# Two attention stages of a two-layer decoder: transposes issued one batch early, a similarity that ends one batch late, and new issue orders for two streams

## What is computed

```
qkv = (x @ W_qkv).reshape(B, N, 3, H, D)          # H 16 heads of D 16
q, k, v = qkv[:, :, 0], qkv[:, :, 1], qkv[:, :, 2]
q_n  = q[:, REG:] / norm(q[:, REG:])              # REG = 5 register tokens
sim  = (qg_n * q_n).sum(-1).mean(-1)              # likeness to a guide vector
sim  = (sim - sim.min()) / (sim.max() - sim.min())  # over all batches
pos  = sim > 0.9
x_pos = attend(q, k, v, keys = registers and tokens with pos)
x_neg = attend(q, k, v, keys = registers and tokens without pos)
reg_out = (x_pos[:, :REG] + x_neg[:, :REG]) * 0.5
tok_out = where(pos, x_pos, x_neg)[:, REG:]
return concat(reg_out, tok_out) @ W_proj + b_proj
```

## Time and profile before

| what | value |
|---|---|
| median of 3 runs (lowest to highest) | 1870.96 us (1869.15 to 1871.81) |
| profiled execution, its own time | 1873.72 us |
| its span in the trace | 1871.5 us |
| mean granted TensorE clock | 0.929 of 2.4 GHz |
| PE busy | 1573.7 us (84%) |
| DVE busy | 973.5 us (52%) |
| ACT busy | 639.9 us (34%) |
| POOL busy | 433.5 us (23%) |

### The profile page before, as it was taken

The page is one execution under the profiler, slowest core; times in us unless marked ns, Lnnn a source line. Parts: engine busy times, 40 slices in busy tenths (PEclk is TensorE's granted clock), DMA queues, the critical chain, the costliest instruction groups (busy, mean ns, idle before and its releaser), DMA issues.

```text
span 1871.5 us, 29566 instructions
## 1 busy us (share of the span) xinstructions
PE 1573.7 (84%) x12928; PEld 1288.5 (69%) x12928; DVE 973.5 (52%) x1774; ACT 639.9 (34%) x710; POOL 433.5 (23%) x403
## 2 busy tenths in 40 slices
PE   6898999988899999999669968977977982787785
PEld 5787888877688888888647756755864762455453
DVE  4666667665353333333455564565655443565654
ACT  4444534344322332322134424424423420323322
POOL 2220202102233443533302320331250232000000
PEclk9999999999789999999889989989989985879878
DMA  5000000000400010100000000000000001101000
GB/s 210 1 1 1 1 1 1 1 1 15 188 18 18 18 34 18 34 1 1 1 1 1 18 18 1 1 34 1 1 34 1 1 17 68 52 1 52 7 13 12
DMA packets 8625, 42.09 MB, mean 22 GB/s; under 512 B 1073, under 2 KB 3377, under 8 KB 7473
## 3 DMA queue, kind: packets, MB, share of 16 engines
q1 hardware_dynamic: 8496, 40.21, 5.7%
HBM read 31.82 MB, written 8.39 MB: 21 GB/s over the span
## 4 chain that ended last, share of the span: by engine, by line
PE 65%; DVE 21%; ACT 7%; POOL 3%; issue 3%; DMA 1%; SPq 0%; DVEq 0%; POOLq 0%; ACTq 0%
PE ps L111 14%; PE ps L112 13%; PE ps L113 13%; DVE sm L1219 8%; PE ps L519 4%; PE ps L793 4%; DVE m L1208 4%; PE ps L524 3%; PE ps L811 3%; ACT m L1124 3%; PE ps L531 3%; PE ps L651 2%; PE ps L817 2%; ACT m L951 2%; PE ps L635 2%
## 5 line engine op out<-in xcount | busy, mean ns | idle before, releaser
L951 ACT ACTIVATE m<-ps 128x1024 f32<-128x1024 f32 (+5 forms) x232 | 179.9, 800 | 416.2 <-PE ps L113 226.1
L1219 DVE TENSOR_REDUCE sm<-ps 128x8 f32<-128x2048 f32 (+1 forms) x128 | 195.8, 1530 | 87.1 <-PE ps L793 74.2
L1208 DVE TENSOR_TENSOR m<-m,ps 128x1024 f32<-128x1024 f32 (+1 forms) x80 | 91.1, 1139 | 219.3 <-PE ps L113 190.3
L519 PE MATMUL ps<-cst,m 128*77 128x128 f32 (+2 forms) x1008 | 144.7, 289 | 53.5 <-DVE m L1599 24.7
L519 PEld LDWEIGHTS ps<-cst,m 128*77 128x77 f32 (+2 forms) x1008 | 120.0, 152 | 83.2 <-issue 32.4
L1746 POOL TENSOR_TENSOR r<-m,r 128x1024 fp32r<-128x1024 f32 x48 | 115.2, 2401 | 264.4 <-ACT r L951 264.4
L1124 ACT ACTIVATE m<-ps 128x2048 f32<-128x2048 f32 x64 | 119.2, 1876 | 164.0 <-PE ps L811 164.0
L1679 POOL TENSOR_SCALAR sm<-sm 128x2 f32<-128x2 f32 x40 | 8.9, 223 | 646.7 <-DVE sm L1237 646.7
L111 PE MATMUL ps<-xTall,uw 128*128 128x512 f32 x384 | 152.5, 397 | 6.4 <-DVE xres L1208 5.0
L112 PE MATMUL ps<-xTall,uw 128*128 128x512 f32 x384 | 152.0, 396 | 0.0
L113 PE MATMUL ps<-xTall,uw 128*128 128x512 f32 x384 | 151.2, 394 | 0.0
(11 more groups left out here) (179 smaller groups left out, 3749.3 us busy)
## 6 DMA issues: line engine op xcount, KB each, us to landing
raw<-wu_dram SPq DMA_DIRECT2D x12, 768.0 KB, 4.2
keep_dram<-m SPq DMA_DIRECT2D x8, 768.0 KB, 3.3
m<-keep_dram SPq DMA_DIRECT2D x8, 768.0 KB, 4.2
w1raw<-w_dram SPq DMA_DIRECT2D x1, 3840.0 KB, 14.5
w0raw<-w_dram SPq DMA_DIRECT2D x3, 1024.0 KB, 19.4
w1f<-w1f_dram SPq DMA_DIRECT2D x1, 2048.0 KB, 18.9
out_dram<-xres SPq DMA_DIRECT2D x16, 128.0 KB, 1.8
w0f<-w0f_dram SPq DMA_DIRECT2D x1, 1536.0 KB, 14.3
```

What stands on the lines that cost most here:

```text
L519: return pe.transpose(o, i, ident[0:n, 0:n])
L951: return act.activation(o, i, ACT.Copy)
L1208: return dve.tensor_tensor(o, a, b_, op)
L1219: return dve.tensor_reduce(o, i, AX.X, op, **kw)
```

## The change

1. **LAST, early transposes.** A generator `early(st, b)` on PE and ACT issues the first part of batch b+2 within the end of batch b: half of the q heads (`tqa`, into bank 3) behind t3, `tk` behind oT, the other q heads and `xt` behind y. The product y goes to bank 2 in place of bank 1. A batch then begins with `xm`, behind `add` of the stream's batch before.
2. **LAST, registers ahead of scores.** `xo` stands behind t2, ahead of s0, and its copy goes from DVE to ACT. The transpose of it has a signal of its own (`x3`). DVE runs xr, xn, xc ahead of rc and on; xc halves as it copies, and one instruction `ov` adds half of the ordinary rows. `oh` is gone.
3. **SECOND, the similarity ends in the next batch.** `likeness` (sc, sim) of batch b-2 is issued behind the rotary embedding of batch b; the last two batches end it in place. POOL's clearing of the head tiles of b+2 (`blank`) stands in `fq(b)` ahead of bias and pow.
4. **SECOND, split transposes.** The transposes of token half 0 wait for t0 alone, the rest for t1. The first values product `v0` of `xattn` stands between oT and y of `a1`.
5. **Both cross attentions.** DVE runs sums 0, sums 1, shift 2, shift 3 in place of sums 0, shift 2, sums 1, shift 3. `maxima_of` and `attend` have no slot end ahead of their first step.
6. **All order tables are new.** Those of PE in LAST, then `early` on PE, and DVE's `likeness`, its place in `a1`, and the new `ov`:

```
 LAST = {
-    "PE": [12, 12, 12, 13, 13, 15, 15, 15, 16, 16, 18, 19, 20, 21, 22, 22, 23, 23, 24, 24, 25, 26, 30, 31, 36, 38, 39, 40],
+    "PE": [5, 5, 6, 6, 6, 7, 8, 10, 11, 12, 14, 14, 16, 16, 18, 20, 22, 23, 23, 25, 25, 27, 27, 30, 30],
...
+            def early(st, b):
+
+                v, sig, act_, dve_ = f_views(st, b), st.f_pe, st.f_act, st.f_dve
+                pe.wait_ge(*st.f_pool.at("clean"))
+                pe.wait_ge(*dve_.at(b, "f"))
+                turn_heads(bank(st, 3), v, 0, [0, 1], [0, 1]).then_inc(sig.up(b, "tqa"), 1)
+                yield
+                if b >= 2:
+                    pe.wait_ge(*dve_.at(b - 2, "on"))
+                turn_heads(pair(st, 0), v, 16, G4, [0, 1]).then_inc(sig.up(b, "tk"), 1)
+                yield
+                pe.wait_ge(*act_.at(b, "Tk"))
+                turn_heads(bank(st, 1), v, 8, [0, 1], [0, 1]).then_inc(sig.up(b, "tq"), 1)
+                pe.wait_ge(*dve_.at(b, "xq"))
+                for c in range(4):
+                    m = tp(bank(st, 0)[:, 32 * c:32 * c + 8], v.qs[:, 4 * c:4 * c + 4, :].rearrange("p h n -> p (h n)"), 8)
+                m.then_inc(sig.up(b, "xt"), 1)
...
+            def likeness(st, b):
+                sig, qq, dq = st.q_dve, k2(st.sm[:, 32:64]), k2(st.sm[:, 64:96])
+                dve.wait_ge(*st.q_pool.at(b, "pow"))
+                tt(dq, dq, qq, ALU.mult).then_inc(sig.up(b, "sc"), 1)
+                yield
+                dve.wait_ge(*sig.at(b, "sc"))
+                reduce(sim[:, 2 * b:2 * b + 2], dq, ALU.add).then_inc(sig.up(b, "sim"), 1)
...
                     tt(v.QK[:, j, :, 0:16], v.t1[:, j, :, :], v.t2, ALU.add).then_inc(sig.up(b, f"t{j}"), 1)
                 yield
+                yield from likeness(st, b - 2) if b >= 2 else pause(1)
+                yield
                 yield from maxima_of(st, b, v, sig, pe_)
...
-                dve.wait_ge(*sig.at(b, "xc"))
-                tt(ov, ov, v.os[0:REG, :, :], ALU.add).then_inc(sig.up(b, "ov"), 1)
-                dve.wait_ge(*sig.at(b, "ov"))
-                ts(v.o[0:REG, 0, :], v.o[0:REG, 0, :], 0.5, None, ALU.mult).then_inc(sig.up(b, "oh"), 1)
+                dve.wait_ge(*sig.at(b, "on"))
+                stt(ov, ov, 0.5, v.os[0:REG, :, :], ALU.mult, ALU.add).then_inc(sig.up(b, "ov"), 1)
```

More of the change, by code:

```diff
@@ L44 @@
+    "POOL": [4, 4, 4, 4, 10, 10, 12, 13, 13, 13, 13, 13, 15, 16, 17, 17, 17],
 }
 SECOND = {
[L46 to L47 removed]
@@ L55 @@
+    "DVE": [4, 5, 5, 5, 6, 7, 9, 11, 13, 14, 15, 15, 15, 16, 16, 20, 20, 22, 22, 22, 25, 30, 31, 31, 31, 31, 31],
 }
@@ L1181, in fa @@
                 v, sig, pe_, dve_ = f_views(st, b), st.f_act, st.f_pe, st.f_dve
[L1182 to L1187 removed]
+                if b < 2:
+                    for _ in early(st, b):
+                        pass
                 yield
@@ L1191, in fa @@
                 yield
+                act.wait_ge(*pe_.at(b, "xo"))
+                copy(v.ox_[:, :, 0:8], bank(st, 0)[:, 0:32].rearrange("p (c n) -> p c n", c=4)).then_inc(sig.up(b, "xo"), 1)
                 yield
                 yield from attend(st, b, v, sig, pe_)
+                nxt = early(st, b + 2) if b + 2 < B else iter(())
+                yield
+                next(nxt, None)
                 yield
@@ L1333, in xattn @@
                 sums(0)
+                sums(1)
                 shift(2)
-                sums(1)
                 shift(3)
@@ L1535, in fq @@
                 yield
-                dve.wait_ge(*st.q_pool.at(b, "pow"))
-                tt(dq, dq, qq, ALU.mult).then_inc(sig.up(b, "sc"), 1)
-                yield
-                dve.wait_ge(*sig.at(b, "sc"))
-                reduce(sim[:, 2 * b:2 * b + 2], dq, ALU.add).then_inc(sig.up(b, "sim"), 1)
+                if b + 2 >= B:
+                    for _ in likeness(st, b):
+                        pass
                 yield
@@ L1776, in a1, with blank @@
             def a1(st, b):
+                sig = st.a_pool
+                yield from blank(st, b) if b < 2 else pause(1)
+                yield
+                add_bias(st, b, part(w1f, P1F, "bao"), st.a_pe, sig)
+                yield
+                yield from norm_only(st, b + 2) if b + 2 < B else pause(4)
+                yield from layernorm(st, b, st.a_dve, sig)
+                yield
+            def blank(st, b):
                 v, sig = a_views(st), st.a_pool
@@ L1787, in a1 @@
                 z.then_inc(sig.up(b, "z"), 1)
-                yield
-                add_bias(st, b, part(w1f, P1F, "bao"), st.a_pe, sig)
-                yield
-                yield from norm_only(st, b + 2) if b + 2 < B else pause(4)
-                yield from layernorm(st, b, st.a_dve, sig)
-                yield
             def fq(st, b):
@@ L1797, in fq @@
                 qq = k2(st.sm[:, 32:64])
+                yield
+                yield from blank(st, b + 2) if b + 2 < B else pause(1)
                 yield
```

182 lines of the change are left out of this document (106 added, 76 removed).

## The result

The changed kernel takes 1793.58 us (median of 4 runs, 1792.77 to 1799.51) against 1870.06 for the kernel before (4 runs, 1862.82 to 1871.81). The ratio is 0.9605, 95% interval 0.9572 to 0.9638: 4% faster, 76 us by the medians, where 63 were forecast. The predicted 1808 is 14 above the measured time, inside the range and inside the likeliest case's own. All times and ratios here are of fast runs; experiment E6 had two slow ones more (2647.0 and 2926.1 us at a granted clock of 0.55 and 0.81), which are left out.

What follows compares the result with a forecast made beforehand. Chains of waits were taken to bound LAST, and SECOND partly. SECOND -35, LAST -27 and FIRST -1 made -63 on the profiled 1873.7, so 1810.7, or 1808 us by the median; range 1782 to 1848.

Steps and rivals of the forecast that it cites:

- likeliest case: Whole kernel: the gains come as laid out, 1808 us, with a range of its own of 1790 to 1826; chance 0.55.
- SECOND, -35: SECOND: pairs of 145 us instead of 153.3 and the last pair's lag gone (-16); bounds -15 to -54.
- The layout: SECOND's pair from its first x transposes: maxima turned at 41, attention to 60, y at 67, 76.7 of PE work left.
- the 8 us of the order: SECOND: shortening of a pair by the in-step order, 153.3 to 145; waits freed by `likeness` were not added.
- LAST, -27: LAST: pairs of 69, 65 and 65 us from xm to xm, last stretch 71.7; bounds -11 to -42.
- two streams side by side fit into 4.77: Attention steps: both streams' steps come back after 4.77 us like one stream's alone, four steps in 19.1 us.
- the 4 us set aside for the clock: LAST: 4 us added to the 60 to 61 laid out for a pair at the higher clock, giving 65.
- FIRST, -1: FIRST: reordered sums and shifts and a few PE products gain 1 us; bounds -5 and +5.
- Rival B: SECOND: like beside like gives nothing, the period stays 153 and only the end gains (-15): 1828 us; chance 0.17.
- C: SECOND and LAST: short steps with waits run at the lower clock, 28 to 35 us lost: about 1840; chance 0.13.
- E: SECOND and LAST: granted clock falls to 1.2 GHz in nearly all attention steps, kernel slower: 1877 us; chance 0.07.
- D: SECOND: late `pow` holds DVE's maxima some 4 us in each of four pairs: 1823 us; chance 0.05.

Runs made afterwards that it cites:

- E6: Kernel before, with the new LAST and SECOND's old code run with its streams in step; FIRST as before: 1869.0 us (ratio 1.0016).
- E4: Changed kernel, but every similarity ends in its own batch, order tables kept: 1836.8 us (ratio 0.9827).
- E11: Changed kernel, but POOL's clearing of the head tiles is back at the start of self attention, behind `pow`: 1824.5 us (ratio 0.9760).
- E5: Changed kernel, but SECOND's two streams in the order of the kernel before, stream 1 half a batch behind: 1851.7 us (ratio 0.9930).
- E1: Kernel before with the change in LAST alone (early transposes, registers ahead of scores, new order tables there): 1853.2 us (ratio 0.9930).
- E3: Changed kernel, but FIRST's order tables and the order of sums and shifts in both cross attentions as before: 1803.3 us (ratio 0.9646).

## Why the prediction was right, and where its sum was off

- **What bounds it**: right. Chains of waits bounded LAST and in part SECOND, and three quarters or more of the gain are idleness of PE (39.7 of 52.7 us in SECOND, 19.4 of 24.2 in LAST). The rest is shorter busy time, which went with a higher granted clock; the sum counted no gain of that kind.
- **The sum as a whole**: by the spans -79.9 for the forecast -63. SECOND gave 17.7 more than its term, LAST 2.8 less, and the part up to SECOND 2.7 more, which is within the scatter of that place; 0.7 was lost between the stages.
- **SECOND, -35, measured -52.7.** This is the term that was mis-sized. The layout put the end of y at 67; its own parts behind the attention steps add up to 5.9, not 7, so it stood at 66. The attention steps began at 40.9 (laid out: 41) but took 22.0 and not 19.1, and y ended at 69.1. That is 2 us worse than laid out. Against it, PE had by then done 54.9 us of the pair's work, not 50, and the pair's PE time was 124.6, not 126.7, so 69.6 were left and not 76.7: pairs of 140.6 and 139.9, not 145. The first pair gained 2.3 and did not lose 1, and the fourth (160.2 with an end of some 20) gained about 9 and not 4. The end itself was right: 35.7 to 20.
- **`likeness` and `blank`, counted at nothing beside the order**: wrong as a price, right in the sum. The forecast took their waits as part of the 8 us of the order. E4 and E11 show 38 and 28 us in SECOND when one of them is undone, E6 a loss when all are. The layout had them in place, so it came out right; as reasons they stood too low.
- **LAST, -27, measured -24.2.** xm to xm was 68.9, 65.0, 65.6 (laid out: 69, 65, 65) and the last stretch 74.2 and not 71.7. The step "two streams side by side fit into 4.77" failed: 5.39. The pair came out at 65.0 all the same, since the 4 us set aside for the clock happened to cover what went over. Up to the end of the attention steps it took 52.4 for the laid out 48 (30.1 up to s0, at a granted clock of 0.72, and 22.3 behind it, at 1.00); from there to the next xm it took 12.6 for 12 to 13. How much of the 4.4 is the clock is not shown, and the match to the microsecond is partly luck. In the last stretch stream 1's y ended 68.0 behind xm, where the layout has 67, and the residual, norm and store behind it took 6.2, for which the sum left 4.7.
- **FIRST, -1**: no effect that these traces can show.
- **Rival B** (like beside like gives nothing): fell for this code, 140.6 against 153.2 in E5. It holds for the old code in the one order in step that was tried, 160.1 in E6 against 153.3. So the rule of the Trainium skill (Perfetto Trace Analysis, Optimization Strategy), that interleaving regimes of different engines may improve performance, is borne out by the runs only where the chains' gaps stay in the code; with the gaps closed, like beside like is the shorter.
- **C and E** (clock): SECOND was granted 0.95 (before 0.93), LAST 0.84 (before 0.82). No loss in the mean of either stage. **D** (`pow` holds the pair): 14.3 us of waits are left, 11 of them in the last pair, where the similarity is in place.

Not settled: what sets the scatter of LAST's 273.7 to 277.9 us between traces of the same instructions. In E1 and E3, with 277.9 and 276.8, 2.7 and 3.7 of it are in the first pair (71.6 and 72.6 for 68.9), whose first xm took 1.17 us there and 0.73 in the changed kernel, and the granted clock of the stage was 0.82 for 0.84. No run separates cause from effect.

## What to carry to other kernels

Price an order of streams and the code that it runs with together. Here both halves of a change were worth nothing or a loss, in two stages, and the whole was worth 53 and 24 us. The reading that fits the traces: with a lag, one stream's waits are covered by the other's work, and closing them bought nothing (13.9 us fewer waits for `pow` in E5, the same SECOND); in step they are the other stream's waits too. This holds for the orders that were tried; a better one for either half by itself was not looked for. When two streams run in step, look first at every wait that both have at the same place, and at what of the other stream is queued behind it on each engine; an edit there can be worth more than its own length (two waits for `pow`, 11.1 us together, cost 13.5 in E4's second pair; one wait of 5.59 on DVE cost 8 to 10 in E11's).

## What the runs showed that was not expected

- Two streams that alternate the four-step loop in the same banks come back after 5.39 us, where one alone does after 4.77: the engine with two steps in the loop, PE, sets it by its fixed order.
- Where SECOND begins differs by up to 10.1 us (914.5 to 924.6) between executions of kernels with the same instructions up to there, so a difference of a few us of one profile at a late place needs a start of its own.
- The granted clock moved with the edits: the same 4208 matmuls of SECOND were busy for 496.1 us at 0.95 in the changed kernel, and for 515.3 at 0.92 in E5. A quarter of SECOND's gain is of this kind, and no term of the forecast stood for it.
